# Order of the last weight loads of a two-block Perceiver kernel: latent attention's weights beside the second cross-attention

## The reference, cut to what matters

```python
x = x + _L0_xattn_ref(_layernorm(x), ctx_2048, ...)                    # X0
x = x + _L0_attn_ref(_layernorm(x), ...)                               # A0
x = x + _L0_ffn_ref(_layernorm(x), ...)                                # F0
x = x + _L1_xattn_ref(_layernorm(x), ctx_2048, mask_BxS2_ik0, ...)     # X1
x = x + _L1_attn_ref(_layernorm(x), wq_down, q_norm_w, wq_up, wq_rope,
                     wkv_down, kv_norm_w, wkv_up, wk_rope, wo)         # M1
x = x + _L1_ffn_ref(_layernorm(x), w_fc, w_proj)                       # F1
```

```python
# X1, for each batch: 16 heads of 16, keys and values from that batch's context
q, k, v = proj(hs, Wq, bq, S), proj(at, Wk, bk, T), proj(at, Wv, bv, T)
probs = softmax(where(attend, clip(q @ k.T / 4, -50, 50), -10000.0))
delta = (probs @ v) @ Wo.T + bo
# M1, latent attention: 16 heads, 128 without and 64 with rotation, latents of 192 and 64
q_c, kv_c = _rmsnorm(x @ wq_down, q_norm_w), _rmsnorm(x @ wkv_down, kv_norm_w)
q_nope, q_rope = q_c @ wq_up, _apply_rope(q_c @ wq_rope)
k_nope, v = split(kv_c @ wkv_up); k_rope = _apply_rope(x @ wk_rope)
out = softmax(causal((q_nope @ k_nope.T + q_rope @ k_rope.T) * scale)) @ v
return out.reshape(bs, s, -1) @ wo
```

## Time and profile before

| what | value |
|---|---|
| runs, us | 674.01, 677.02, 678.55 |
| median, us | 677.02 |
| span of the profiled execution, us | 676.7 |
| TensorE clock granted, mean | 0.995 |
| TensorE busy | 641.7 us, 95% |
| VectorE busy | 427.2 us, 63% |
| ScalarE busy | 273.3 us, 40% |
| data moved by DMA | 42.25 MB |

### The profile page before, as it was taken

How to read it: one execution, slowest core, us unless ns; L and a number is a source line. 1 busy time by engine, 2 the same in 40 slices (tenths; PEclk the granted TensorE clock), 3 DMA queues, 4 the chain that set the end, 5 groups by cost and what they waited for, 6 DMA issues and landing times.

```text
span 676.7 us, 21596 instructions
## 1 busy us (share of the span) xinstructions
PE 641.7 (95%) x9572; PEld 429.4 (63%) x9572; DVE 427.2 (63%) x998; ACT 273.3 (40%) x502; POOL 62.0 (9%) x132
## 2 busy tenths in 40 slices
PE   8999999999978999999999999999989999999876
PEld 4666666666656566666666566766657775455654
DVE  4544567686754655555553863554768985687687
ACT  2454544445432234334334744444243554011134
POOL 1020000000000111101110013001200202000000
PEclk9999999999998999999999999999999999999999
DMA  7252112117006301000003511100293100000000
GB/s 237 63 164 65 34 33 64 34 34 220 2 3 236 108 32 33 32 15 20 1 2 100 214 62 32 65 34 33 60 248 101 64 4 1 2 3 3 3 1 32
DMA packets 42365, 42.25 MB, mean 62 GB/s; under 512 B 15904, under 2 KB 33056, under 8 KB 42016
## 3 DMA queue, kind: packets, MB, share of 16 engines
q1 hardware_dynamic: 42272, 40.86, 19.4%
HBM read 40.33 MB, written 0.52 MB: 60 GB/s over the span
## 4 chain that ended last, share of the span: by engine, by line
PE 77%; DVE 14%; issue 4%; ACT 2%; SPq 1%; DMA 1%; POOL 0%; DVEq 0%; POOLq 0%; ACTq 0%
PE psum L387 14%; PE psum L379 14%; PE psum L1119 7%; PE psum L454 5%; PE psum L429 4%; PE psum L1170 4%; PE psum L1125 4%; PE psum L419 3%; PE psum L1844 2%; PE psum L404 2%; PE psum L1821 2%; PE psum L1868 2%; PE psum L1140 2%; PE psum L1154 1%; PE psum L1098 1%
## 5 line engine op out<-in xcount | busy, mean ns | idle before, releaser
L387 PE MATMUL psum<-arena 128*128 128x256 f32 x512 | 121.5, 384 | 2.0 <-DVE arena L659 1.4
L379 PE MATMUL psum<-arena 128*128 128x512 f32 x256 | 121.5, 602 | 1.1 <-DMA arena<-in_ctxT 1.1
L387 PEld LDWEIGHTS psum<-arena 128*128 128x128 f32 x512 | 93.9, 190 | 23.8 <-issue 9.0
L379 PEld LDWEIGHTS psum<-arena 128*128 128x128 f32 x256 | 44.8, 190 | 44.5 <-issue 42.7
L674 ACT ACTIVATE arena<-arena 128x512 f32<-128x512 f32 x64 | 47.9, 804 | 50.5 <-DVE arena L798 50.5
L1119 PE MATMUL psum<-y_cols,arena 128*128 128x512 f32 x112 | 52.9, 605 | 0.0
L668 ACT ACTIVATE arena<-psum,arena 128x512 f32<-128x512 f32 x64 | 40.2, 687 | 31.0 <-DVE arena L785 30.9
L454 PEld LDWEIGHTS psum<-arena 128*17 128x17 f32 x4096 | 38.5, 96 | 22.2 <-issue 16.9
L798 DVE TENSOR_SCALAR arena<-psum 128x512 f32<-128x512 f32 x64 | 39.7, 682 | 14.5 <-PE psum L419 10.5
L1222 ACT ACTIVATE arena<-psum 128x512 f32<-128x512 f32 x48 | 28.5, 597 | 48.9 <-PE psum L1119 30.9
L785 DVE TENSOR_REDUCE arena<-psum 128x1 f32<-128x512 f32 x64 | 39.7, 682 | 12.8 <-PE psum L404 12.5
(11 more groups left out here) (248 smaller groups left out, 957.6 us busy)
## 6 DMA issues: line engine op xcount, KB each, us to landing
arena<-in_ctxT SPq DMA_DIRECT2D x32, 512.0 KB, 3.6
arena<-in_L_attn_Wv SPq DMA_DIRECT2D x1, 2048.0 KB, 8.3
arena<-in_L_attn_Wq SPq DMA_DIRECT2D x8, 256.0 KB, 2.9
arena<-in_L_attn_Wk SPq DMA_DIRECT2D x8, 256.0 KB, 3.2
arena<-in_L_attn_Wo SPq DMA_DIRECT2D x1, 2048.0 KB, 11.3
arena<-in_L_ffn_w_gating SPq DMA_DIRECT2D x1, 2048.0 KB, 7.7
arena<-in_L_attn_wo SPq DMA_DIRECT2D x2, 1024.0 KB, 5.5
arena<-in_wq_upT SPq DMA_DIRECT2D x2, 768.0 KB, 7.4
```

What stands on the lines that cost most here:

```text
L379: last = nc.tensor.matmul(bank, wkv[:, c, i * P:(i + 1) * P], x[:, c, :], start=(c == 0), stop=(c == NC - 1))
L387: last = nc.tensor.matmul(bank[:, kk * D:(kk + 1) * D], x[:, c, k * P:(k + 1) * P], wkv[:, c, D:2 * D], start=(c == 0), stop=(c == NC - 1))
```

## The change

Only SP's program changes. Before, none of M1's weights is issued until batch 13's context, where SP waits for `s_pv` at 28; then `load` and the first half of the heads go out, the second half beside batch 14, the first up half beside batch 15, and the other three large pieces behind the loop, at `s_pv` 36, 40 and 44.

After, the up halves go out beside the contexts of batches 9 and 10 and the out halves beside 11 and 12, with no wait but `done[F0]`. Behind the loop come the heads' halves at `s_pv` 32 and 36, and `load`, with its sixteen small transfers, last, at `s_pv` 40. The same 28 transfers are issued, with the same shapes, sources and places.

```diff
-                    if b == 13 and ph(M1):
+                    if b == 9 and ph(M1):
                         sp.wait_ge(done[F0], 1)
-                        sp.wait_ge(phases[X1].s_pv, 4 * 7)
-                        phases[M1].load(sp)
-                        phases[M1].load_heads(sp, 0)
-                    elif b == 14 and ph(M1):
-                        phases[M1].load_heads(sp, 1)
-                    elif b == 15 and ph(M1):
                         phases[M1].load_up(sp, 0)
+                    elif b == 10 and ph(M1):
+                        phases[M1].load_up(sp, 1)
+                    elif b == 11 and ph(M1):
+                        phases[M1].load_out(sp, 0)
+                    elif b == 12 and ph(M1):
+                        phases[M1].load_out(sp, 1)
                 phases[X1].load_later(sp, 2, beside_x1)
                 if ph(M1):
+                    sp.wait_ge(phases[X1].s_pv, 4 * 8)
+                    phases[M1].load_heads(sp, 0)
                     sp.wait_ge(phases[X1].s_pv, 4 * 9)
-                    phases[M1].load_up(sp, 1)
+                    phases[M1].load_heads(sp, 1)
                     sp.wait_ge(phases[X1].s_pv, 4 * 10)
-                    phases[M1].load_out(sp, 0)
-                    sp.wait_ge(phases[X1].s_pv, 4 * 11)
-                    phases[M1].load_out(sp, 1)
+                    phases[M1].load(sp)
```

## The result

The changed kernel took 681.62 us, median of 18 runs (678.51 to 684.17), beside 678.46 us for the kernel before, median of 18 (673.97 to 681.03). The ratio is 1.0051, 95% interval 1.0034 to 1.0068: 3.5 us slower. (The ratio is estimated from all runs; the two medians differ by 3.2 us.) The forecast was no difference, 677.0 us, range 672.4 to 680.8. A half percent is under what I had called tellable; with 18 runs on each side it is clear of zero.

What follows compares the result with a forecast made beforehand. The prediction took the kernel as bound by TensorE's work, busy 95% of the span, with the moved loads hidden. Its five terms of 0 us summed to 0 us, so it forecast 677.0 us, range 672.4 to 680.8 us.

Steps and rivals of the forecast that it cites:

- The four large pieces sooner: Up and out halves issued earlier in X1: loads already hidden with 21 us of slack before `fold`, so 0 us.
- Contexts 10 to 13 behind the pieces: Contexts with a large piece ahead on the queue: queue empty again before each next context, so 0 us.
- Context 14: Freed of the small transfers, goes out at an estimated 488 us, about 8 us sooner; nothing waited for it, 0 us.
- The heads and small transfers last: Issued behind X1's last contexts, all landed by 531.4 us, 19 us of slack before `fold`: 0 us.
- The traffic moves: DMA traffic leaves 484 to 510 us and joins turns 1, 2, 4 and 5 of X1: 0 us.
- Two of the signs: Named as proving it wrong: stops without releaser in turns 1 to 5; turn 9's stop and the span both going.
- The stop in turn 9: TensorE's 1.64 us stop in the value products, taken as alignment and unchanged: 0 us, bounds -1.64 to +0.56 us.
- The new traffic: Loads beside the value products of turns 1, 2, 4 and 5: 0 us, upper bound one stop of 2.20 us.
- The first rival: Bigger bursts stop TensorE's instructions in value products of turns 1, 2, 4, 5: 8.8 us slower, 685.8 us; chance 0.05.
- The rival of the late small weights: `load` lands 19 us later than expected and `fold` waits: 677 us plus little; chance 0.01.
- the faster one: Calmer traffic from 484 to 531 us removes 4.5 us of TensorE's waits: 672.5 us; chance 0.08.

Runs made afterwards that it cites:

- e2: Kernel before with up halves beside batches 13 and 14, then heads, out halves, small transfers last, nothing early: ratio 0.9979, 1.4 us faster.
- e3: Changed kernel with its out halves one batch later, beside batches 12 and 13, nothing large beside batch 11: ratio 1.0006 to the kernel before.
- e4: Changed kernel with GpSimd's reduction one place later, behind the mask product of batch 5: ratio 0.9978 to the kernel before, 1.5 us faster.
- e6: Changed kernel with out halves beside batches 9 and 10 and up halves at 13 and 14: ratio 1.0016 to the kernel before, 1.1 us slower.
- e8: The version e2 with GpSimd's reduction also one place later: ratio 0.9967 to the kernel before, 2.2 us faster.
- e9: Changed kernel with its four early pieces at batches 10 to 13 and GpSimd's reduction one place later: ratio 0.9959 to the kernel before, 2.8 us faster.
- e5: Kernel before, loads unchanged, with GpSimd's reduction one place later, behind the mask product of batch 5: ratio 0.9973, 1.8 us faster.
- e1: Kernel before with only the first out half (1024 KB) moved, to beside batch 11's context: ratio 1.0039, 2.6 us slower.
- e7: Kernel before with both out halves (2048 KB) moved to beside batch 11's context: ratio 1.0080, 5.4 us slower.

## Why the prediction was wrong

**What held.** The four large pieces sooner: 0 us. TensorE waits for no DMA from 400 to 560 us, before or after, and `fold`, `down` and VectorE's guest find their weights there. The issue times were right once the shift of the trace is taken off (427.11 - 1.5 = 425.6 us). Contexts 10 to 13 behind the pieces: 0 us. Context 14 went out at 493.33 us, less the shift of 5.6 us 487.7, forecast 488. The heads and small transfers last: e2 shows that this order costs nothing. Its sixteen issues took 12.6 us instead of 10.85, inside the slack of 19.

**What failed is the part "The traffic moves", twice, and a term that was missing.** Two of the signs that the prediction had named for being wrong are there: a stop without a releaser in turn 2, and the stop of turn 9 gone (though the span grew). The measured 681.62 us is 0.8 us over the range. Part of that is the low base: the same rule with the highest of the eighteen runs, 681.03 + 2.20, would have held it. The mechanism would have been wrong all the same.

*The stop in turn 9.* I took it as alignment, because a stop of 2.20 us in X0 had idle DMA engines beside it, and left it at 0 us. It gave 1.80 us back. e2, e3, e4, e6, e8 and e9, with less traffic before it, don't have it; e5, with the loads of before, has it at 1.6 us. But e1 and e7 keep the traffic of turn 9 and have 0.8 us and none. What tells them apart is when the instruction packet comes: before, it starts at 503.48 us, with the value products at 503.38; in e1 0.5 us ahead of them (506.20 and 506.69); in e7 2.3 us ahead (504.16 and 506.48). The stop in X0 ends 1.3 us behind such a packet too (197.84 to 198.85, then 200.15), with no data beside it. So the two stops are alike in what TensorE waits for, as their place had suggested; the inference from idle DMA engines in X0 to a stop that the moved loads can't change was the mistake. Why the packet in X0 comes late stays open.

*The new traffic.* I took 0 us, with one stop of 2.20 us as the bound; it is one stop that costs 1.68 us. The first rival had named the mechanism and four places for it in the value products; it came in one place, in the scores of turn 2, which I hadn't looked at. e6 and e9 tie it to the piece beside batch 9: 1.0 to 1.2 us with 512 KB (the change, e3, e4), 1.9 us with 1024 KB, none when the piece stands one batch later. That TensorE lacks instructions there is read from the packets above: in the change, e3 and e6 the packet starts where the queued data end, within 0.02 us. The Trainium skill, "DMA: Bandwidth & Descriptors", section "Queues, rings and completion order", has the engines take turns between queues packet by packet; in these three traces no such turn is seen. The Trainium skill, "Runtime: NRT & Kernel Launch", section "Instruction fetch mechanics", calls the crossing of a block mostly hidden; it was not here, where one crossing cost 1.68 us.

*The missing term.* TensorE's longest wait in the stretch was for GpSimd, 1.9 us, and I passed over it because its releaser is no DMA. I never asked what kept GpSimd; the sum left this wait unchanged without a reason. It was the reduction, just behind the issue of batch 11's context, and the change put 1 MB beside it. e1 has a longer wait and a loss with that piece alone, e3 removes both by moving the piece, e4 and e5 together by moving the reduction, and e7 makes both larger with the dose. In the change's trace it is 0.84 us of wait and 1.61 us of lower clock, 2.45 us; the two stops almost cancel (1.68 and -1.80). By e3, e4 and e5 it is about 3 of the 3.5 us. How much of it is wait and how much clock over all runs is not shown.

The rival of the late small weights didn't come about, nor did the faster one: its waits for VectorE and ScalarE, 1.4, 0.9 and 0.6 us, stand unchanged.

## What to carry to other kernels

When transfers are moved, ask of every wait beside their new place what slows the engine that is waited for, and not only whether a DMA is the releaser: a wait that exists already has no cover, and what is added to it can reach the end in full (it did in e7: the wait 3.2 us longer, X1 in the trace 3.2 us longer, with 1.6 us of clock lost and 1.6 us of stop gained). A reduction across partitions on GpSimd is best placed where nobody waits for what stands behind it in GpSimd's program, and away from large transfers. Early is no gain for a load with 20 us of slack; where it must go somewhere, try it one loop turn earlier and later: moving two pieces by one turn (e3) was worth about 3 us here. A stop without a releaser is worth holding against the instruction packets in the trace's DMA records.

## What the runs showed of the hardware

From GpSimd's reduction across partitions of two columns to its next instruction the profile shows 6.7 to 7.2 us of idle time beside 512 KB of DMA, 7.0 us beside 1 MB, 8.0 and 8.5 us beside 1.5 MB (at most 7.7 us in e4) and 10.4 us beside 2.5 MB, although its data lie in SBUF and the transfers write other words. Which part of it the traffic slows is open.

TensorE stopped where a 16 KB packet of its instructions came late: each of the 43 stops in eleven traces ended 1.2 to 1.6 us after such a packet had. In three traces the packet started only when the data queued before it had ended (432.01, 431.16 and 430.67 us).

A granted clock of 1.2 GHz for most of 3.5 us followed an idle TensorE of 2.7, 1.9 and 5.1 us in three profiles (the change, e6, e7), and did not follow 3.2 us in a fourth (e1), nor the 1.9 us in the kernel before. In X0 a stop of 2.2 to 2.7 us near 198 us stands in all eleven profiles, and in all of them the clock from 198 to 220 us is below full, at 0.77, 0.84 or 0.92.
